# Deformable convolution after whitening: another order of the twelve sampling matmuls of a step

## What is computed

```
om      = conv3x3(x, w_off) + b_off        # 27 planes per image
py, px  = om[:9]  + row + ky,  om[9:18] + column + kx
mask    = sigmoid(om[18:])
sampled = mask * bilinear(x, py, px)       # 9 taps per output pixel, each channel
out     = einsum('bckhw,ock->bohw', sampled, w) + b
out     = relu(batchnorm(out)) + x
```

## Time and profile before

| what | value |
|---|---|
| median of three runs | 2130.82 us |
| the profiled execution | 2128.34 us |
| its span, first to last instruction | 2126.5 us |
| mean granted TensorE clock | 0.865 of full speed |
| main loop, first to last copy of L866 | 564.8 to 1892.0 us, 464 copies |
| PE busy in the span | 75% |
| DVE busy in the span | 76% |
| ACT busy in the span | 68% |

### The profile page before, as it was taken

How to read it: one execution, slowest core, us unless ns; L and a number is a source line. 1 busy time by engine, 2 the same in 40 slices (tenths; PEclk the granted TensorE clock), 3 DMA queues, 4 the chain that set the end, 5 groups by cost and what they waited for, 6 DMA issues and landing times. The chain is left out here.

```text
span 2126.5 us, 63487 instructions
## 1 busy us (share of the span) xinstructions
PE 1587.5 (75%) x24974; PEld 1087.2 (51%) x24975; DVE 1622.4 (76%) x2176; ACT 1443.3 (68%) x2225; POOL 636.1 (30%) x1200
## 2 busy tenths in 40 slices
PE   4767453120399999999999999999999999961710
PEld 3644221010276666666766766666666667640310
DVE  5344587495599999999989999999999999962205
ACT  1211226245499999999999999999999999950102
POOL 3000111100234444434444444444444344410000
PEclk9679776665599999999999999999999999995555
DMA  3075368777757776676676676776776777730008
GB/s 127 0 198 140 87 230 282 204 271 255 234 133 165 164 159 159 155 160 158 159 169 149 158 164 155 158 172 162 159 155 154 161 163 159 161 55 4 0 4 368
DMA packets 291492, 333.27 MB, mean 157 GB/s; under 512 B 73736, under 2 KB 265609, under 8 KB 289163
## 3 DMA queue, kind: packets, MB, share of 16 engines
q1 hardware_dynamic: 240550, 260.38, 46.1%
q0 software_dynamic: 48128, 67.28, 14.1%
q10 hardware_dynamic: 2534, 1.72, 0.4%
HBM read 230.42 MB, written 98.63 MB: 155 GB/s over the span
## 5 line engine op out<-in xcount | busy, mean ns | idle before, releaser
L152 POOL DMA_DIRECT2D rows<-scratch_parts x1152 | 588.4, 519 | 730.2 <-PE ps_even_y L764 707.5
L914 DVE TENSOR_TENSOR G<-odd_y,ps_odd_v 128x504 f32<-128x504 f32 (+2 forms) x928 | 571.7, 658 | 93.7 <-PE ps_odd_v L794 58.6
L794 PE MATMUL ps_odd_v<-tent_x,stage 32*128 32x171 f32 (+1 forms) x5568 | 636.2, 323 | 0.0
L860 ACT COPY odd_y<-ps_odd_y 128x504 f32<-128x504 f32 (+2 forms) x928 | 526.6, 567 | 62.2 <-PE ps_odd_y L773 24.7
L773 PE MATMUL ps_odd_y<-rows,sel 32*128 32x504 f32 (+2 forms) x928 | 459.7, 495 | 119.0 <-ACT sel L842 105.0
L794 PE MATMUL ps_even_v<-tent_x,stage 32*128 32x171 f32 (+3 forms) x5568 | 534.2, 322 | 13.1 <-ACT even_v L866 12.7
L923 DVE TENSOR_TENSOR G<-even_v,ps_even_y 128x1008 f32<-128x1008 f32 (+2 forms) x464 | 538.9, 1161 | 1.2 <-ACT even_v L866 0.9
L794 PEld LDWEIGHTS ps_odd_v<-tent_x,stage 32*128 32x128 f32 x5568 | 507.9, 186 | 0.0
L794 PEld LDWEIGHTS ps_even_v<-tent_x,stage 32*128 32x128 f32 x5568 | 420.5, 186 | 155.6 <-issue 150.5
L812 PE MATMUL ps_r<-G,conv_w 128*32 128x224 f32 (+1 forms) x8832 | 475.9, 342 | 0.7 <-ACT res L871 0.7
L866 ACT COPY even_v<-ps_even_v 128x1008 f32<-128x1008 f32 (+2 forms) x464 | 451.0, 972 | 19.5 <-PE ps_odd_v L794 9.6
(11 more groups left out here) (134 smaller groups left out, 960.1 us busy)
## 6 DMA issues: line engine op xcount, KB each, us to landing
place<-scratch_om SPq DMA_DIRECT2D x960, 105.0 KB, 3.5
rows<-scratch_parts POOLq DMA_DIRECT2D x960, 52.5 KB, 3.6
scratch_parts<-high SPq DMA_DIRECT2D x16, 1764.0 KB
scratch_parts<-tent_y SPq DMA_DIRECT2D x16, 1764.0 KB
place<-scratch_om SPq DMA_DIRECT2D x192, 84.0 KB, 2.7
scratch_om<-om SPq DMA_DIRECT2D x64, 165.4 KB
rows<-scratch_parts POOLq DMA_DIRECT2D x192, 42.0 KB, 2.8
scratch_conv<-res SPq DMA_DIRECT2D x448, 14.0 KB, 2.0
```

Source lines behind the costliest of these rows:

```text
L152: eng.dma_start(bass.AP(tensor=rows[b][:].tensor, offset=32 * g * pitch + here, ap=[[2 * pitch, Y_KINDS], [GROUP * W, 3], [1, count * W]]) ...
L794: m = nc.tensor.matmul(sub(ps_v[g // 2], 0, 128, i * 512 + lo + first, dims), stage[32 * g:32 * g + 32, j * IMAGE + v * C:j * IMAGE + (v + ...
L860: nc.scalar.copy(odd_y[p % 3][:, i * ROW + lo:i * ROW + hi], ps_odd_y[:, lo:hi]).then_inc(odd_kept, 1)
L914: nc.vector.tensor_tensor(sub(G, 0, 128, slot(v) + i * ROW + lo, [[1, hi - lo]]), odd_y[p % 3][:, i * ROW + lo:i * ROW + hi], ps_v[1][:, i ...
```

## The change

The twelve sampling matmuls get an order written out by hand, as pairs (quarter, column span). Before, they ran over j and within it over g: (0,0) (1,0) (2,0) (3,0), then the first odd spread of the next step, then (0,1) (1,1) (2,1) (3,1) (0,2) (1,2) (2,2) (3,2). Now three come ahead of the spread, (0,0) (1,0) (3,0), and nine behind it: (0,1) (1,1) (3,1) (2,0) (0,2) (2,1) (1,2) (2,2) (3,2). Quarter 2 has three matmuls, as before; its first one now stands behind the spread too. The number of instructions, the waits and their values and the last matmul, which increments `sampled`, stay the same.

```diff
--- before.py
+++ after.py
@@ -661,6 +661,7 @@
                                  "odd_weighted", "even_weighted")]
             reduced, res_ready = sem("reduced"), sem("res_ready")
             res_stored = [sem(f"res_stored{b}") for b in range(2)]
+            SAMPLING = ((0, 0), (1, 0), (3, 0), (0, 1), (1, 1), (3, 1), (2, 0), (0, 2), (2, 1), (1, 2), (2, 2), (3, 2))
             ASKED = {first + count - 2: n for n, (first, count) in enumerate(BATCHES)}
             block = st.enter_context(nc.Block())
 
@@ -780,20 +781,19 @@
                             pe.wait_ge(stage_loaded[c], 16 * 4 * len(COLUMNS) * (it + 1))
                     pe.wait_ge(tent_ready, n + 1)
                     wait(pe, even_kept, n)
-                    for j, (x0, x_lo, x_hi) in enumerate(COLUMNS):
-                        if j == 1 and to:
+                    for at, (g, j) in enumerate(SAMPLING):
+                        if at == 3 and to:
                             rows_ready(*to)
                             spread_odd(*to, 0)
                         first, count = SPAN * j, min(SPAN, W - SPAN * j)
-                        for g in range(4):
-                            i, v = g % 2, 2 * p + g // 2
-                            if j == 0 and g >= 2:
-                                wait(pe, odd_weighted, 2 * n - 1 + i)
-                            lo, hi = columns(v)
-                            dims = [[W, (hi - lo) // W], [1, count]]
-                            m = nc.tensor.matmul(sub(ps_v[g // 2], 0, 128, i * 512 + lo + first, dims),
-                                                 stage[32 * g:32 * g + 32, j * IMAGE + v * C:j * IMAGE + (v + WIN) * C],
-                                                 sub(tent_x[p % 3], 32 * g, 32, lo + first, dims), start=True, stop=True)
+                        i, v = g % 2, 2 * p + g // 2
+                        if j == 0 and g >= 2:
+                            wait(pe, odd_weighted, 2 * n - 1 + i)
+                        lo, hi = columns(v)
+                        dims = [[W, (hi - lo) // W], [1, count]]
+                        m = nc.tensor.matmul(sub(ps_v[g // 2], 0, 128, i * 512 + lo + first, dims),
+                                             stage[32 * g:32 * g + 32, j * IMAGE + v * C:j * IMAGE + (v + WIN) * C],
+                                             sub(tent_x[p % 3], 32 * g, 32, lo + first, dims), start=True, stop=True)
                     m.then_inc(sampled, 1)
 
                 def reduce(it, blk, t):
```

## The result

The changed kernel takes 2168.76 us in the median (2166.97 to 2171.47) against 2131.24 us for the kernel before on the same chip (2126.55 to 2135.06). The ratio is 1.018, with a 95% interval from 1.015 to 1.020: slower by 33 to 43 us. The profiled execution took 2171.47 us, 2169.7 of it the span. The main loop, from the first to the last copy of L866, went from 564.7 to 1933.4 us, 1368.7 us long; before it was 1327.2. So the loop is 41.5 us longer, and the span as a whole 43.2: the change sits where the edit is. The mean granted TensorE clock of the span is 0.865 in both profiled executions.

A forecast was written before the change was run, and what follows sets the result against it. Bound after the change: a ring through ACT's copy, the spread and quarter 2's passes, 2.66 + 0.32 = 2.98 us a step. 3.0 us a pair times 16 is 48, taken as 46: 2176 us, range 2155 to 2196.

The forecast's parts named there:

- The ring: From ACT's keep_even over its odd-spread copy, PE's next spread and quarter 2's passes to keep_even: 2.66 us before, 2.98 after.
- the step laid bare: Main-loop step without a reduce, bound by ACT's copy, the spread and quarter 2's passes: 2.66 us before the change.
- signs of being wrong: Spread starting clearly after the copy's end, a ps_odd_v tail pass taking other than 0.16 us, or (3,0) holding the spread.
- The rule on weight loads: On TensorE, loads overlap a running matmul only across row groups; both added passes at 0.25 us, 2252 us in all.
- No other ring in its place: Main loop: PE no longer bounds any full step and DVE (2.72 us) idles, so the period is 2.98 in all.
- (3,0) at nothing: (3,0), just ahead of the spread, waits for DVE's second L914; released 0.15 us before the spread's own wait, cost nothing.
- The sum: Main loop: 2.5, 0.32 and 0.2 us, together 3.0 a pair, times 16 pairs 48 us, taken as 46.
- The edges of a pair: The first and the last two steps of a pair, with short views: 0 give or take 0.2 us.
- The first pair: Some steps of the first pair of images wait for transfers and hide part of their loss: 48 us becomes 46.
- DVE at 2.72 us a step: DVE needs 2.72 us from one L914 pair to the next, with no idle time shown: nearly a bound.
- Faster: Rival: the spread's earlier place outweighs (2,0), until DVE's 2.72 us bounds the step: 2070 us, half of it 2100; chance 0.08.
- No difference: Rival: PE starts (2,0) before the waiting spread, or records are another quarter's; order hardly matters: 2130 us; chance 0.06.

The follow-up runs named there:

- the run with the half copy: Changed kernel with ACT's copy of image 1's odd spread cut to half its columns from the seventh step on: 2112.40 us, ratio 0.992.
- the run with both orders: Changed order only in steps sampling after the reduce of 24 matmuls (and steps 0 and 4), otherwise the kernel before: 2121.76 us, ratio 0.995.
- the fastest kernel: Changed kernel with a separate semaphore for keep_even, (3,0) behind the spread, (1,2) ahead of (2,1), odd_y buffers by step number: 2088.20 us, ratio 0.979.

## Why the prediction was right, and where its numbers were off

**The ring.** It was forecast at 2.98 us and measured at 2.96 and 2.95. Term by term from the rows of after: 0.90 to the copy, 0.58, 0.06, 0.33, then 0.74 for the five starts from the first to the last pass of quarter 2, 0.29 and 0.06. Against the step laid bare in the earlier trace rows all terms but one are the same within 0.01. That one is the passes, 0.74 for five or 0.148 each, where the prediction had 0.46 + 0.32 = 0.78, with 0.16 for a pass from the nearest row; with the two added passes at 0.148 the sum is 2.96. By its letter one of the prediction's signs of being wrong came up, a pass that takes another time than 0.16; it is the size of a term and not the mechanism. The other signs came as foretold: idle time of 133.5 us before L914 (about 140), 124.9 before L866 (over 100), less before L860. That the ring closes as described is shown from five sides: the passes (quarter 2 twice), the copy (half of it), the way back to `keep_even` (its own semaphore), the place of (2,0) (put back), and the counter-proof in the order of before, where neither the copy nor the semaphore did more than 0.3%, and the copy shortened the one step that the ring bounds there.

**The rule on weight loads** was weighed against the trace: a load overlaps a running matmul only when the row group is another ("TensorE: Matmul & The Clock Gate", Part 3, in the Trainium skill). Six passes in one row group at 0.148 us each, where the first pass behind a cold load needs 0.25, speak against it for this kernel. Its time would have been 2252 us.

**No other ring in its place.** The prediction worked out that PE's chain would fall behind in every full step, even in that with 24 reduce matmuls. It did: 3.16 us became 2.96. Sampling starts at T + 1.15 in an ordinary step (1028.01), not at T + 1.04. This fits its wait for `even_kept`, as `keep_even` ends at 1027.86; the prediction had looked at the reduce alone. It changes nothing, since both lie ahead of T + 1.53.

**(3,0) at nothing.** The 0.15 us to spare that were worked out are 0.16 in the rows of after, and the run with the half copy shows them used up.

**The sum** was 46 us. The medians differ by 37.5 (33 to 43), and the loop in the profiles grew by 41.5. Of the terms, the price of a pass accounts for most: 25 full steps in 16 pairs, 400 times about 0.025 us, is 10 us too much. The other way, the second semaphore wait behind ACT's copy was overlooked; five full steps a pair at 0.065 are 5 us. The edges of a pair were taken as 0 give or take 0.2 us and came out at -0.2, which is another 3 us too much: the first step of a pair got shorter, from 2.91 to 2.72 us. The step near the end became 0.19 longer, as forecast. That makes 48 - 10 + 5 - 3 = 40.

The first pair was read wrongly. The prediction took 2 us off because some of its steps "wait for transfers and would hide part of theirs". They don't: PE, ACT and DVE wait for each other in them too, as everywhere in the loop. They run at the lower of the two levels of TensorE's clock, a granted clock of 0.50 (1.2 GHz), up to 586 us before and 588 us after; then it is 1.00. Before, and after:

```profile
571.65 1.00 ACT L866 COPY even_v<-ps_even_v 128x1008 f32<-128x1008 f32 x1 [0.55 <-PE ps_odd_v L794]
...
575.32 1.00 ACT L866 COPY even_v<-ps_even_v 128x1008 f32<-128x1008 f32 x1 [0.55 <-PE ps_odd_v L794]
```

```profile
568.20 1.00 ACT L866 COPY even_v<-ps_even_v 128x1008 f32<-128x1008 f32 x1 [0.97 <-PE ps_odd_v L794]
...
572.25 1.00 ACT L866 COPY even_v<-ps_even_v 128x1008 f32<-128x1008 f32 x1 [1.12 <-PE ps_odd_v L794]
```

A step went from 3.67 to 4.05 us, 0.38 more instead of the 0.18 of the same steps at full clock. The first pair grew by 4.0 us and the usual one by 2.5, so these steps add 1.5 us where 2 were taken off, and the 40, which hold neither, become 41.5, the growth of the loop. The errors of the terms partly cancel, so that the total is off by less than the largest of them. The rest is scatter between executions.

The upper end of the range, 2196, doesn't follow from its own terms: 0.18 for a pass is 16 us above 2176, and 8 more make 2200. Nothing hangs on it.

**DVE at 2.72 us a step** was a bound that isn't one. The earlier trace rows shows a pair starting 2.72 us after the last with no idle time, but with the ring open pairs follow at 2.62: the next starts 0.33 us after the start of `cap`, before the 0.42 of its record are over (1025.32, 1025.65). In the 2.72 there was some 0.1 us of waiting that overlapped the end of `cap` and so did not count as idle. It entered only the rival's price: 2070 was forecast for a loop bound by DVE.

**The rivals.** Faster was to be decided by whether ACT's copy is through before sampling starts. In the fourth step it is, and there the changed order helps, as the run with both orders shows: by 0.11 us in most blocks, 0.5% in all (0.2 to 0.7). No difference is refuted by the result, and by the matmul put back.

## What to carry to other kernels

Before work is moved behind an instruction that waits, ask whether that wait lies on a ring, and how long the ring is with the moved work in it; a step in which the other bounds happen to be absent, here the one without a reduce, shows the bare ring for reading. Work ahead of a wait is free up to the wait's length and dear on either side of it. And where a consumer waits for the last of several results but reads only some, a semaphore for these can open the ring: here it turned a loss of 1.8% into a gain of 1.0%, and with an order made for it into one of 2.1%, while that order without the semaphore lost 1.7%, and the semaphore in the order of before gained 0.2%.

## What the runs showed of the hardware

- The row groups of TensorE run each at its own pace. Two passes more cost 139 us in the row group of the ring and 7 us in another, where of the full steps only those behind the reduce of 24 matmuls grew, by 0.02 to 0.13 us.
- Matmuls of different row groups don't start in program order, but their increments come in it. The last matmul of a step is one of quarter 3. Its last record goes from 1029.27 to 1029.57, while quarter 2's last pass starts at 1029.47 and ends at 1029.76. The trace has the increment at 1029.79, 0.03 us after that, and `keep_even` starts at 1029.82. The increment on (1,2) in the changed order came 0.03 us after the last pass of (2,1).
- A weight load of PE that waits for two semaphores started 0.11 us after the later event, one that waits for one 0.05 to 0.06.
- Six passes of 171 and 162 columns in one row group, each with its own weight load, start 0.148 us apart.
- Operations of DVE that follow each other overlap at their ends by about 0.08 us (the records of a step in the fastest kernel, 1.27, 1.20 and 0.42 us, add up to 2.89, and the step lasts 2.64). Starts, not records' ends, tell how long an engine needs.
- At the lower level of the granted clock (0.50) a step of the changed kernel lasted 4.05 us, at the full one 2.96.
